# Attention weights turned by DMA transposes from SP in place of TensorE transposes

## The reference, cut to what matters

```python
x = x + autocorrelation(layernorm(x), ctx, ctx)        # 8 x 512 x 2048, here the "attention stage"
x = x + ffn(layernorm(x))                              # 2048 x 2048 weights and LoRA adapters

def autocorrelation(Q, K, V):                          # for each batch, each of the 2048 channels
    corr = ifft(fft(q) * conj(fft(k))).real            # 512 lags
    w, idx = top_k(corr, 12)                           # the 12 largest lags
    w = softmax(w)
    out = sum_i w_i * v[min(idx_i + pos, 511)]
```

## Time and profile before

| | |
|---|---|
| median of 3 runs | 3153.94 us (3153.56 to 3158.97) |
| the profiled execution | 3155.11 us, its span 3153.3 us |
| PE busy | 3046.3 us, 97% |
| DVE busy | 2077.2 us, 66% |
| POOL busy | 1688.5 us, 54% |
| ACT busy | 1118.0 us, 35% |
| granted TensorE clock | 0.987 of full speed over the span |
| attention stage | about the first 1660 us, 32 groups |

### The profile page before, as it was taken

One profiled execution on the slowest core, in us unless ns is written; L12 is line 12 of the kernel. 1 busy time (PEld: TensorE's weight loads), 2 busy tenths in 40 slices (PEclk: granted clock), 3 DMA queues, 4 the chain that ended last, 5 costly groups with the idle time before them and its releaser, 6 DMA issues. The chain is left out here.

```text
span 3153.3 us, 37958 instructions
## 1 busy us (share of the span) xinstructions
PE 3046.3 (97%) x14387; PEld 1642.8 (52%) x14387; DVE 2077.2 (66%) x2735; ACT 1118.0 (35%) x1696; POOL 1688.5 (54%) x759
## 2 busy tenths in 40 slices
PE   5999999999999999999977999999999999999999
PEld 3566565665656566566633444444444444444444
DVE  5899998999989999899984444443544444344321
ACT  4666665666656666555521110110111011011100
POOL 6798898988979898898751211221122122112210
PEclk8999999999999999999988999999999999999999
DMA  6334344343444534434259434344343534444321
GB/s 229 127 106 167 131 154 157 113 167 135 149 159 145 174 132 152 152 112 153 80 181 277 139 112 146 103 129 150 107 128 110 160 91 134 144 117 127 94 74 40
DMA packets 280787, 430.26 MB, mean 136 GB/s; under 512 B 147440, under 2 KB 163952, under 8 KB 265072
## 3 DMA queue, kind: packets, MB, share of 16 engines
q1 hardware_dynamic: 145456, 394.43, 36.1%
q10 hardware_dynamic: 135168, 33.57, 5.9%
HBM read 308.15 MB, written 86.25 MB: 125 GB/s over the span
## 5 line engine op out<-in xcount | busy, mean ns | idle before, releaser
L1402 PE MATMUL ps<-w_hi,h_hi 128*128 128x512 f16 x2048 | 777.0, 379 | 2.3 <-DVE xt L1509 2.2
L1403 PE MATMUL ps<-w_lo,h_hi 128*128 128x512 f16 x2048 | 776.6, 379 | 0.0
L1404 PE MATMUL ps<-w_hi,h_lo 128*128 128x512 f16 x2048 | 776.4, 379 | 0.0
L1282 POOL TENSOR_TENSOR xt<-xt,vl 128x2048 f32<-128x2048 f32 x31 | 139.6, 4503 | 921.4 <-DMA xt<-x_scratch 676.5
L877 PE MATMUL ps<-op,it 128*128 128x512 f32 x1024 | 447.5, 595 | 12.8 <-DVE op L1023 12.8
L802 PE MATMUL ps<-wt,fp 128*128 128x512 f16 x1536 | 338.6, 380 | 1.4 <-DVE wt L990 1.4
L1402 PEld LDWEIGHTS ps<-w_hi,h_hi 128*128 128x128 f16 x2048 | 200.6, 98 | 242.6 <-issue 10.5
L1404 PEld LDWEIGHTS ps<-w_hi,h_lo 128*128 128x128 f16 x2048 | 200.5, 98 | 242.0 <-issue 0.6
L877 PEld LDWEIGHTS ps<-op,it 128*128 128x128 f32 x1024 | 195.1, 191 | 247.5 <-issue 230.9
L1403 PEld LDWEIGHTS ps<-w_lo,h_hi 128*128 128x128 f16 x2048 | 200.5, 98 | 230.8 <-issue 0.3
L802 PEld LDWEIGHTS ps<-wt,fp 128*128 128x128 f16 x1536 | 150.7, 98 | 184.2 <-issue 2.5
(11 more groups left out here) (184 smaller groups left out, 5735.3 us busy)
## 6 DMA issues: line engine op xcount, KB each, us to landing
sg<-lora_ab SPq DMA_DIRECT2D x112, 512.0 KB, 4.8
cg<-ctx SPq DMA_DIRECT2D x32, 1024.0 KB, 5.2
xv<-x SPq DMA_DIRECT2D x32, 1024.0 KB, 5.2
x_scratch<-xv SPq DMA_DIRECT2D x32, 1024.0 KB, 6.4
xt<-x_scratch SPq DMA_DIRECT2D x32, 1024.0 KB, 5.0
out<-xt SPq DMA_DIRECT2D x32, 1024.0 KB, 3.9
xg<-x SPq DMA_DIRECT2D x30, 1024.0 KB, 8.4
xrow<-x SPq DMA_DIRECT2D x24, 1024.0 KB, 5.8
```

The lines of the kernel that those rows point to most:

```text
L1282: nc.gpsimd.tensor_tensor(xt[:, k, :], xt[:, k, :], vl[:, :], ALU.add).then_inc(vl_ok, 1)
L1402: nc.tensor.matmul(ps[:, c, :], h_hi[k][:, i, :], w_hi[c][:, i, :], start=(i == 0), stop=False)
L1403: nc.tensor.matmul(ps[:, c, :], h_hi[k][:, i, :], w_lo[c][:, i, :], start=False, stop=False)
L1404: last = nc.tensor.matmul(ps[:, c, :], h_lo[k][:, i, :], w_hi[c][:, i, :], start=False, stop=(i == KT - 1))
```

## The change

The 16 TensorE transposes of a group go. The split is made while the channels are still on the partitions: ACT writes the high part of `wd` to `w16[0]` (`high_of_w`), DVE the rest to `w16[1]` (`w_rest`), both fp16 in SBUF, in memory of `mi`. SP then issues four DMA transposes (high part and rest, two channel blocks each, 128x1024 fp16) into `wt`, whose layout is now block, lag part, channel. `weight_spectra` waits for those four (`s_wt`) in place of `wt_lo`, and reads `wt` with a strided pattern. DVE makes the split for group n+1 right behind `top_lags(n+1)` and ahead of `add_output(n)`; before, it stood at the start of the next step, behind `add_output(n)`. ACT does `sum_of_weights` ahead of `sums_of_top` and `divide_w`. The three tiny steps that bound the FFN weights (`bound_of_w`) are the same instructions. SP's loop over batches 1 to 3 is written out.

```diff
-            wt = sb("wt", [P, 2, 4, GC], FP16, st)
+            wt = sb("wt", [P, 2, CT, 4, P], FP16, st)
+            w16 = [mi[:, 2 * k:2 * k + 2, :].rearrange("p a c -> p (a c)").bitcast(FP16).rearrange("p (j c) -> p j c", c=L) for k in range(2)]
...
+                    def turn_weights(b, g):
+                        n = GPB * b + g
+                        if later(b, g):
+                            sp.wait_ge(w_spec, 8 * n)
+                        for a, split in enumerate((wt_hi, wt_lo)):
+                            for k in range(2):
+                                sp.wait_ge(split, 4 * n + 2 * k + 2)
+                                sp.dma_start_transpose(wt[:, a, 2 * k:2 * k + 2, :, :].rearrange("p j l c -> p (j l) c"),
+                                                       w16[a][:, 2 * k:2 * k + 2, :].rearrange("p j l -> p (j l)")).then_inc(s_wt[a][k], 16)
...
                         if convert:
                             store_weights(b, g, 1)
+                        if lead:
+                            turn_weights(*ahead(b, g, 1))
...
-                    with sp.Fori(1, B // 2) as b:
+                    for b in range(1, B // 2):
...
-                    def transposed_out(b, g):
+                    def high_of_w(b, g):
                         n = GPB * b + g
-                        if later(b, g):
-                            act.wait_ge(w_spec, 8 * n)
-                        for k in range(4):
-                            act.wait_ge(wt_spec, 4 * n + k + 1)
-                            nc.scalar.activation(wt[:, 0, k, :], ps[:, k, :], ACT.Copy, scale=WSCALE).then_inc(wt_hi, 1)
+                        for j in range(CT):
+                            act.wait_ge(w_ready, 4 * n + j + 1)
+                            nc.scalar.activation(w16[0][:, j, :], wd[:, j, :], ACT.Copy, scale=WSCALE).then_inc(wt_hi, 1)
...
+                        if not convert:
+                            sum_of_weights(b, g)
                         if lead:
                             sums_of_top(*ahead(b, g, 1))
                             divide_w(*ahead(b, g, 1))
-                        if not convert:
-                            sum_of_weights(b, g)
...
                     def weight_spectra(b, g, lead):
                         n = GPB * b + g
-                        pe.wait_ge(wt_lo, 4 * n + 4)
+                        pe.wait_ge(w_ready, 4 * n + 4)
+                        for a in range(2):
+                            for k in range(2):
+                                pe.wait_ge(s_wt[a][k], 16 * n + 16)
                         for i in range(4):
-                            forward_pair(i, (ER, EI)[i % 2], (wt[:, 0], wt[:, 1]), i // 2).then_inc(w_spec, 1)
+                            forward_w(i, (ER, EI)[i % 2], i // 2).then_inc(w_spec, 1)
...
                     def step(b, g, more, lead, scale=False):
-                        transpose_w(b, g, scale)
+                        if scale:
+                            bound_of_w()
                         if lead:
                             q_spectrum(*ahead(b, g, 1))
...
                     def w_rest(b, g):
                         n = GPB * b + g
-                        if later(b, g):
-                            dve.wait_ge(w_spec, 8 * n)
-                        for k in range(4):
-                            dve.wait_ge(wt_hi, 4 * n + k + 1)
-                            nc.vector.scalar_tensor_tensor(out=wt[:, 1, k, :], in0=ps[:, k, :], scalar=WSCALE, in1=wt[:, 0, k, :],
+                        for j in range(CT):
+                            dve.wait_ge(wt_hi, 4 * n + j + 1)
+                            nc.vector.scalar_tensor_tensor(out=w16[1][:, j, :], in0=wd[:, j, :], scalar=WSCALE, in1=w16[0][:, j, :],
                                                            op0=ALU.mult, op1=ALU.subtract).then_inc(wt_lo, 1)
...
                     def step(b, g, lead, convert, first=False):
-                        w_rest(b, g)
                         if lead:
                             corr_products(*ahead(b, g, 1))
...
                             top_lags(*ahead(b, g, 1), (b, g) if convert else None, None if convert else (b, g))
+                            w_rest(*ahead(b, g, 1))
```

More of the change, by code:

```diff
@@ L285, in build @@
             w_ready = sem("w_ready", st)
-            wt_spec = sem("wt_spec", st)
+            s_wt = [[sem(f"s_wt{a}{k}", st) for k in range(2)] for a in range(2)]
             wt_hi = sem("wt_hi", st)
@@ L386, in step @@
                             store_weights(b, g, 1)
+                        if lead:
+                            turn_weights(*ahead(b, g, 1))
+                        if convert:
                             if lead:
@@ L418, in _ @@
                     load_context(0, 3)
+                    turn_weights(0, 0)
                     for g in range(GPB):
                         step(0, g, True, True, True, False, True, False)
-                    with sp.Fori(1, B // 2) as b:
+                    for b in range(1, B // 2):
                         for g in range(GPB):
@@ L704, in step @@
                     def step(b, g, more, lead, far, rows, convert):
-                        transposed_out(b, g)
+                        high_of_w(b, g)
                         if convert:
@@ L804, in forward_pair, with forward_w @@
                         return last
+                    def forward_w(bank, kind, part):
+                        dst = ps[:, bank, :].rearrange("p (j c) -> p j c", c=P)
+                        for k in range(2):
+                            for i, (tab, val) in enumerate(((0, 0), (1, 0), (0, 1))):
+                                last = nc.tensor.matmul(dst, fp[:, tab, k, kind, :], wt[:, val, :, 2 * part + k, :],
+                                                        start=(k == 0 and i == 0), stop=(k == 1 and i == 2))
+                        return last
                     def c_spectrum(b, g):
@@ L829, in q_spectrum, with bound_of_w @@
                             forward_pair(4 + i, i, (qh, ql[k]), i // 2).then_inc(q_spec, 1)
-                    def transpose_w(b, g, scale):
+                    def bound_of_w():
+                        pe.wait_ge(w_ready, 4 * (NG // 2) + 4)
+                        pe.wait_ge(top_ok, 1)
+                        nc.tensor.transpose(ps[0:1, 3, 0:P], wtop[:, 0:1], ident[:, :]).then_inc(top_spec, 1)
+                        pe.wait_ge(row_max, 1)
+                        nc.tensor.matmul(ps[:, 3, P:P + 1], ones[0:1, :], wtop[0:1, 1:2], start=True, stop=True).then_inc(topall_ok, 1)
+                        pe.wait_ge(top_read, 1)
@@ L832, in transpose_w, with weight_spectra @@
+                    def weight_spectra(b, g, lead):
                         n = GPB * b + g
                         pe.wait_ge(w_ready, 4 * n + 4)
-                        if scale:
-                            pe.wait_ge(top_ok, 1)
-                            nc.tensor.transpose(ps[0:1, 3, 0:P], wtop[:, 0:1], ident[:, :]).then_inc(top_spec, 1)
-                        for k in range(4):
[L838 to L844, removed]
@@ L846, in weight_spectra @@
-                    def weight_spectra(b, g, lead):
-                        n = GPB * b + g
-                        pe.wait_ge(wt_lo, 4 * n + 4)
+                        for a in range(2):
+                            for k in range(2):
+                                pe.wait_ge(s_wt[a][k], 16 * n + 16)
                         for i in range(4):
-                            forward_pair(i, (ER, EI)[i % 2], (wt[:, 0], wt[:, 1]), i // 2).then_inc(w_spec, 1)
+                            forward_w(i, (ER, EI)[i % 2], i // 2).then_inc(w_spec, 1)
@@ L851, in weight_spectra @@
                         if lead:
                             pe.wait_ge(cprod, 4 * n + 8)
+                        else:
+                            pe.wait_ge(out_add, 4 * n)
                         for i in range(4):
-                            forward_pair(4 + i, (OR, OI)[i % 2], (wt[:, 0], wt[:, 1]), i // 2).then_inc(w_spec, 1)
+                            forward_w(4 + i, (OR, OI)[i % 2], i // 2).then_inc(w_spec, 1)
                     def correlation(b, g):
@@ L1053, in top_lags @@
                         if later(b, g):
-                            dve.wait_ge(wt_spec, 4 * m)
                             dve.wait_ge(op_sum, 6 * m - 1)
@@ L1118, in _ @@
                     top_lags(0, 0, None, None)
+                    w_rest(0, 0)
                     for g in range(GPB):
```

1 line of the change is left out of this document (removed).

## The result

The changed kernel takes 3379.14 us in the median (3378.3 to 3381.72, 4 runs), against 3156.45 us (3153.56 to 3161.41, 4 runs) for the kernel before in the same comparison: a ratio of 1.0707, 95% interval 1.0693 to 1.0721. It is slower by 7.1%. Its profiled execution took 3378.61 us, with a span of 3376.7 us where before had 3153.3: +223.4 us. The mean granted clock is 0.949, before 0.987.

What follows compares the result with a forecast made beforehand. PE's and DVE's equal chains form a tight ring in the attention stage, neither alone binding. Longer W to S adds 83 + 34 + 122, ends 2: +241 us on 3155.11, 3396; the median lies 1.2 below. Forecast 3392 us, range 3230 to 3470.

Steps and rivals of the forecast that it cites:

- ACT's high part at W + 1.2: W is when a group's weights `wd` are ready; ACT's four high-part copies were to end 1.2 us later.
- The new wait of `q_spectrum` for `add_output`: On PE: with `w_rest` ahead of `add_output` on DVE, `q_spectrum` and all behind it on PE wait for DVE.
- The alternation with POOL: DVE's `w_rest` and POOL's SBUF sums exclude each other; `w_rest` ends at W + 6.0, second half W + 8.3.
- Rival A: Cheap split on DVE: little POOL contention, `w_rest` ends at W + 3.6; +90 us, 3245 us; chance 0.20.
- PE idle some 7 us: PE ahead of `q_spectrum`: idle from W - 0.3 to W + 6.8, in the second half likewise.
- The clock: PE's granted clock falls in each group's gap; 3.7 us at half clock lose 1.85, taken as 2.0 us.
- near 0.93: Sign in the profile after: granted clock over the attention stage, for 4 us at half clock in 57.
- `q_spectrum` of 5.18 us: PE's `q_spectrum`, counted at 5.18 us between W and S, the first matmul of `weight_spectra`.
- Transposes hidden: SP's DMA transposes land at W + 9.3 and W + 11.6, before `q_spectrum` ends at W + 14.0 and W + 16.3.
- rival B: The transposes' landing sets the start of `weight_spectra`: 3445 us, 3775 if serial, 4260 at the extreme; chance 0.16.
- the block price of 41.9 us: The skill's 1309 ns per DMA-transposed block: a group's 32 blocks one by one, 34.7 us past the 7.2 replaced.
- Rivals C and D: C: POOL's sums fall elsewhere, `w_rest` is free, 3104 us, chance 0.04. D: no change within 0.2%, chance 0.02.

Runs made afterwards that it cites:

- e1: The changed kernel with DVE doing `add_output` ahead of `w_rest` again; 3292.51 us, 1.0433 of the kernel before.
- e8: The changed kernel with the weights left in PSUM, so each `w_rest` operation has one SBUF input, not two; 3243.67 us, 1.0284 of the kernel before.
- e3: The changed kernel with 26 unused matmuls of 512 columns on PE in the gap ahead of `q_spectrum`; 3331.98 us, 1.0565 of the kernel before.
- e7: The changed kernel with both rest transposes issued a second time into an unread tile, and PE waiting for them; 3390.41 us, 1.0744 of the kernel before.
- e5: The changed kernel with `add_output` ahead of `w_rest` on DVE and POOL's `fold_q` waiting for the split; 3236.88 us, 1.0262 of the kernel before.
- e10: The changed kernel with weights in PSUM, `add_output` and split interleaved, first high part early, SP's weight load ahead of transposes; 3194.36 us, 1.0126 of the kernel before.
- e9: The changed kernel with `fold_q` behind the split, split and `add_output` interleaved on DVE, first group's high part early; 3211.86 us, 1.0185 of the kernel before.
- e11: e10 with two DMA transposes of 128x2048 in place of four of 128x1024; 3200.11 us, 1.0149 of the kernel before.

## Why the prediction was right, and where it was off

The forecast, 3392 us, lies 13 us above the measured 3379.14, within the range of 3230 to 3470. By its own steps:

1. ACT's high part at W + 1.2: 823.32 + 2.20 is W + 1.27. Right.
2. The new wait of `q_spectrum` for `add_output`: 29 groups, 198.6 us. Right; e1 shows that the order on DVE makes it.
3. The alternation with POOL. `w_rest` ended at W + 5.7 (forecast 6.0) in the first half and at W + 7.8 (8.3) in the second. Right, and e8 shows the cause: one input in PSUM ends it while POOL goes on. Rival A, the cheap split, is refuted by the same rows.
4. PE idle some 7 us: 6.7 in plain groups, 7.9 in groups 4, 8 and 12, and 7.1 in the second half. Right.
5. The clock: 2.0 us taken, 2.1 measured by e3, though not evenly: 1.5 and 2.8 us in turn from group to group. Here the size was right in part by luck: the time at half clock behind the gap was taken from one place alone, and its bounds were 0 and 3.7 us. The sign "near 0.93" is worked out wrongly (4 us at half clock in 57 are 0.965); 0.92 was measured, since the clock is down for 6.8 or 10.2 us a group, part of it in the gap itself.
6. `q_spectrum` of 5.18 us is what e3's sum comes back to.
7. Transposes hidden: in 30 groups of 32. e7 shows it, and with it rival B fails for this order of work. e1, e5 and e10 show that B is next in line: as soon as DVE's part is mended, the landing ends PE's wait in 31 groups. SP's own work moved little here, but the list of what stands behind the transposes on its queue left out the load of `wc`: DVE waits 15.4 us in 4 places for `wch`, before 8.5 in 3, and 55.1 and 54.3 us in 17 places in e1 and e5, where W to S is short. The 7.2 us that the block price of 41.9 us is set against stand in no row: the transposes took 1.97 us, and W to S 7.04.

Rivals C and D needed POOL's phase to move off. It followed S, as the unchanged 42.3 us from S to W show.

The sum of 241 us was 18 too high, and two of its terms were badly sized beneath that. The first group was put at -1 us and measured +8.6, with 1.5 us more behind S. The step that failed is "PE starts `q_spectrum` earlier by the transposes". PE did start it earlier, at 75.25, and ended it 5 us before W; but S then waits for the landing. There ACT's high part stands behind two other pieces of ACT's prologue, DVE is idle for 4.41 us until it comes, its split then alternates with POOL for 9.72 us, and the landing comes last, with no `q_spectrum` to hide it. Changed kernel, DVE and SP, then PE:

```profile
90.17 9.72 DVE L1010 SCALAR_TENSOR_TENSOR mi<-wd,mi 128x512 f16<-128x512 f32 x4 [4.41 <-ACT mi L685]
...
90.69 10.47 SPq L354 DMA_TRANSPOSE wt<-mi  x4
```

```profile
103.13 12.29 PE L824 MATMUL ps<-wt,fp 128*128 128x512 f16 x48 [22.53 <-DMA wt<-mi]
```

I had worked out the steady group and took the first for a shorter one of its kind, without reading ACT's queue in the prologue. The second term is the groups of the second half, 15 x 8.1 = 122 us, measured 96.0 in 14 groups and 2.2 in the last. Part is a slip of the count: 12 + 4 + 15 groups and the two ends are 33, of 32. Part is the kind: groups 17 to 19 keep the pattern of the first half (+4.5, +7.2, +6.0), the last but one added 0.6, and the clock's turns bring the others to some 7 and some 8 us where 8.1 was taken throughout. The 12 plain groups (83 forecast, 80.1 measured) and the 4 others (34, 35.6) were right. So the errors of about +11 and about -26 us partly cancelled: that the total lies within 13 us is in part luck.

## What to carry to other kernels

Moving work off an engine that is the bound gains only if the path through it gets shorter: here 1.97 us of transposes left PE, and the chain put in their place needs W + 7.6 at its best, against W + 7.04 (in the second half 7.8 to 8.4 against 8.16). Before a tile is moved from PSUM to SBUF, look at what the other engines do on SBUF at that moment; the same four operations took 2.47 us or 5.77 us by that alone. Removing work from an engine also removes cover: count the new idle time at what the clock takes back behind it, and work out the first and the last iteration by themselves. And what stands behind the new DMAs on their queue comes later: look at who waits for it.

## What was not expected of the hardware

- The granted clock fell around a gap of PE of 2.14 us in e9, in the windows shown there, while it stayed at 1.00 in one of 2.97 us in the kernel before, and for the 12 us behind it. In e1 and e5 it fell behind some waits of 2.1 to 3.4 us and not behind others alike (in e1 behind one of 3.21 us, and not behind one of 3.23). The length of the gap alone does not tell; what else decides was not settled.
- The loss behind a gap alternates: in the changed kernel `q_spectrum` took 6.69 us behind a gap of 6.68 us, and 7.98 us in the next group behind one of 6.63.
- The time of SP to issue a DMA transpose grows with its size: 1.25 us for 128x1024 fp16, 2.1 us for 128x2048 (e11).
- POOL pays for the contention as well: its sum of 1024 columns took 2.78 us beside the split and 2.34 beside the one of e8.
